# Products of ones in the waits of the head, slot constants computed earlier, and another order of ScalarE's work in the steps, in an attention and expert layer

## The reference

```
xn = layernorm(x)
q, k, v = xn Wq' + bq, xn Wk' + bk, xn Wv' + bv
pq, pk = elu(q) + 1, elu(k) + 1
x = x + (pq * cumsum(pk * v over tokens) / 4) Wo' + bo
xn = layernorm(x)                            # router, experts, shared part read this
top2 of xn @ router_w (8 experts); scores = softmax(top2 logits)
routed = sum over the two experts e of
         score_e * (silu(xn @ w1[e][:, :512]) * (xn @ w1[e][:, 512:])) @ w2[e]
shared = (silu(xn @ w_gate) * (xn @ w_up)) @ w_down       # 1024 wide
out = x + routed + shared
```

## Time and profile before

| | us |
|---|---|
| median of 3 runs | 373.13 (371.63 to 373.34) |
| the profiled execution | 372.15 |
| its span, first to last instruction | 370.4 |
| PE busy | 338.9 (91%) |
| DVE busy | 235.4 (64%) |
| ACT busy | 214.4 (58%) |
| POOL busy | 191.4 (52%) |
| mean granted TensorE clock | 0.984 |

### The profile page before, as it was taken

How to read it: one execution, slowest core, us unless ns; L and a number is a source line. 1 busy time by engine, 2 the same in 40 slices (tenths; PEclk the granted TensorE clock), 3 DMA queues, 4 the chain that set the end, 5 groups by cost and what they waited for, 6 DMA issues and landing times.

```text
span 370.4 us, 9019 instructions
## 1 busy us (share of the span) xinstructions
PE 338.9 (91%) x2868; PEld 251.9 (68%) x2868; DVE 235.4 (64%) x579; ACT 214.4 (58%) x389; POOL 191.4 (52%) x293
## 2 busy tenths in 40 slices
PE   6966698999997999999999899999999999999980
PEld 6755477887885887898888455656655556666650
DVE  4989976696984986887788556454545534443430
ACT  3778639776794776965535444454554554545440
POOL 4823185587786775948143641554343543434332
PEclk9999899999999899999999999999999999999997
DMA  6986162337374563455876345967595777686530
GB/s 186 388 206 202 25 123 73 74 88 230 61 183 159 116 198 75 118 186 160 242 238 157 87 70 92 92 92 105 79 105 84 102 108 83 103 99 96 77 48 0
DMA packets 77467, 46.41 MB, mean 125 GB/s; under 512 B 61040, under 2 KB 72560, under 8 KB 77040
## 3 DMA queue, kind: packets, MB, share of 16 engines
q1 hardware_dynamic: 63088, 35.08, 37.8%
q0 software_dynamic: 9664, 10.71, 19.0%
q10 hardware_dynamic: 4672, 0.07, 1.3%
HBM read 19.09 MB, written 12.97 MB: 87 GB/s over the span
## 4 chain that ended last, share of the span: by engine, by line
PE 51%; POOL 18%; DVE 12%; issue 10%; ACT 5%; DMA 1%; POOLq 1%; DVEq 0%; ACTq 0%
PE bU L1029 13%; PE bG L1029 12%; PE bV L1050 7%; POOL x_rows L571 6%; PE bQ L1050 6%; PE bD L927 3%; PE bU L238 3%; PE bG L238 2%; PE bK L1009 2%; DVE ab L1479 2%; DVE st L1356 2%; POOL y L486 1%; PE bV L238 1%; PE bK L238 1%; ACT xn L1122 1%
## 5 line engine op out<-in xcount | busy, mean ns | idle before, releaser
L1479 DVE SCALAR_TENSOR_TENSOR ab<-bU,sg 128x512 f32<-128x512 f32 x64 | 44.1, 690 | 77.2 <-PE bU L1029 51.3
L762 POOL DMA_INDIRECT out_y<-xs,dst_row x32 | 50.0, 1562 | 62.5 <-DMA out_y<-xs,dst_row 37.5
L1162 ACT ACTIVATE sg<-bG 128x512 f32<-128x512 f32 x64 | 37.9, 592 | 45.4 <-PE bG L1029 26.4
L1029 PE MATMUL bG<-we,work 128*128 (+1 forms) x216 | 52.6, 380 | 0.9 <-DVE wd L1535 0.9
L1029 PE MATMUL bU<-we,work 128*128 (+1 forms) x216 | 52.6, 379 | 0.0
L571 POOL DMA_INDIRECT x_rows<-rows,slot_u x32 | 38.3, 1198 | 21.0 <-DVE slot_u L1530 10.4
L1306 ACT ACTIVATE ws_h<-ab 128x512 f16<-128x512 f32 x36 | 22.7, 629 | 41.5 <-DVE ab L1479 41.5
L1169 ACT ACTIVATE ah<-ab 128x512 f16<-128x512 f32 x32 | 20.1, 628 | 32.7 <-DVE ab L1479 27.7
L1759 DVE TENSOR_TENSOR ws_h<-ab,ws_h 128x512 f16<-128x512 f32 x36 | 24.9, 693 | 20.8 <-ACT ws_h L1306 18.5
L1029 PEld LDWEIGHTS bG<-we,work 128*128 128x128 f16 (+1 forms) x216 | 20.7, 99 | 20.4 <-issue 2.8
L1029 PEld LDWEIGHTS bU<-we,work 128*128 128x128 f16 (+1 forms) x216 | 19.8, 99 | 17.4
(11 more groups left out here) (323 smaller groups left out, 811.0 us busy)
## 6 DMA issues: line engine op xcount, KB each, us to landing
stage<-in_w_expert SPq DMA_DIRECT2D x24, 512.0 KB
we<-in_w_shared SPq DMA_DIRECT2D x3, 1024.0 KB, 11.0
xs<-bo POOLq DMA_DIRECT2D x8, 256.0 KB, 4.1
out_y<-xs SPq DMA_DIRECT2D x8, 256.0 KB, 3.6
xs<-in_x SPq DMA_DIRECT2D x1, 1280.0 KB, 18.2
x_rows<-we SPq DMA_DIRECT2D x9, 134.0 KB
xs<-in_x SPq DMA_DIRECT2D x3, 256.0 KB, 3.8
work<-x_rows SPq DMA_TRANSPOSE x40
```

The lines of the kernel that those rows point to most:

```text
L762: pool.indirect_dma_start(out_rows, bass.IndirectOffsetOnAxis(ap=dst_row[:, b:b + 1], axis=0), ya[b % NY], None, bounds_check=NT * P - 1, ...
L1029: ins = pe.matmul(dst[t * n:(t + 1) * n, :], x2[:, hi * KC + k, t * n:(t + 1) * n], w[t][lo][:, k, half, :], start=s == 0 and k == 0, stop ...
L1162: act.activation(sg[q][:], src[:], ACT.Silu, scale=1.0 / WS).then_inc(S["sg_done"], 1)
L1479: dve.scalar_tensor_tensor(out=ab[q][:], in0=src[:], scalar=1.0 / WS, in1=sg[q][:], op0=ALU.mult, op1=ALU.mult).then_inc(S["a_done"], 1)
```

## The change

The diff, with the code that only gives it context cut:

```
 GpSimd
             add_bo(1)
             norm1(2)
+            slot_constants(0)
             pow2(0)
             add_bo(2)
+            slot_constants(1)
             norm1(3)
             pow2(1)
             gaps(0)
+            slot_constants(2)
             add_bo(3)
             add_taken(0)
             to_rows(0)
...
             gaps(1)
             add_taken(1)
+            slot_constants(3)
             to_rows(1)
             for i in range(3, B):
...
-                if i < 7:
-                    slot_constants(i - 3)
                 to_rows(i - 1)
 TensorE
-            def warm(n):
+            def warm(n, dst=bR):
                 for _ in range(n):
-                    pe.matmul(bR[:, 0:P], ones16[:], ones16[:], start=True, stop=True)
+                    pe.matmul(dst[:, 3 * P:4 * P], ones16[:], ones16[:], start=True, stop=True)
...
   in project(2), ahead of the third pass:       + warm(12, bQ)
   in attend_out(1), ahead of the third pass:    + warm(10)
   in gate_up, n = 2, m = 0, ahead of the third: + warm(16, bT)
             warm(48)
             pe.wait_ge(S["const_pool"], 4)
+            pe.wait_ge(S["pow1"], 1)
+            warm(10)
             turn_first(0)
+            warm(8)
             project(0, "kv")
             turn_first(1)
+            warm(7)
             project(0, "q")
             project(1)
+            warm(16)
             attend_out(0)
             turn_first(2)
+            warm(8, bQ)
             project(2)
+            warm(10)
             attend_out(1)
+            warm(22)
             route(0)
             pe.wait_ge(S["const_pool"], 6)
             gate_up(0, 0)
             gate_up(0, 1)
+            warm(20, bD)
             ranks(0)
...
   in expert_down:
                 pe.wait_ge(S["ath_done"], b + 1)
+                if b == 0:
+                    pe.wait_ge(S["ex_lo"], 3 * E)
   ahead of the blocks:
-            pe.wait_ge(S["ex_lo"], 3 * E)
+            pe.wait_ge(S["ex_lo"], 3 * E - 1)
             for b in range(NBLK):
 ScalarE, in every step
                 act_hi(j, 0)
+                silu(n + 1, 1)
+                act_hi(j, 1)
                 if i < B - 1:
                     normed1(i + 1)
-                silu(n + 1, 1)
-                if i < B - 1:
                     row_hi1(i + 1)
-                act_hi(j, 1)
                 expert_hi(part_of_step(i, first + 1))
 ScalarE, behind the steps, last piece of batch 7
             silu(n + 3, 1, bK)
+            expert_hi(part_of_step(B, 6))
             act_hi(j, 3)
-            expert_hi(part_of_step(B, 6))
 VectorE, the same place
             expert_lo(part_of_step(B, 5))
+            swiglu(n + 3, 1, bV)
             act_lo(j, 2)
-            swiglu(n + 3, 1, bV)
             act_lo(j, 3)
```

More of the change, by code:

```diff
@@ L805, in project @@
                             if s == 2:
+                                if i == 2:
+                                    warm(12, bQ)
                                 pe.wait_ge(S["l1_done"], i + 1)
@@ L826, in attend_out @@
                     if s == 2:
+                        if i == 1:
+                            warm(10)
                         pe.wait_ge(S["cxl_done"], i + 1)
@@ L889, in gate_up @@
                             if s == 2:
+                                if n == 2 and m == 0:
+                                    warm(16, bT)
                                 pe.wait_ge(S["sh_lo"], 3 * (n // 2) + m + 1)
```

11 lines of the change are left out of this document (6 added, 5 removed).

## The result

The changed kernel took 366.97 us (median of 4 runs, 366.93 to 367.03), the kernel before beside it 373.08 (371.63 to 373.34): ratio 0.984, 95% interval 0.982 to 0.987, 6.1 us less. The forecast was 367.1. The profiled execution took 367.03 us with a span of 365.3, 5.1 less than before.

The account below looks back on a forecast made before the run. TensorE was taken as full but with holes ahead of the blocks. Gains of 3.54 + 1.36 + 0 + 0 + 1.15 = 6.05 us gave 367.1 us from the 373.13 median, range 364.9 to 370.8.

Parts of the forecast that it names:

- Step 5 and step 6: Two stretches of TensorE's products ahead of the blocks: silu no longer late, gaining 3.54 us and 0.86 us.
- Start of the blocks: First expert product no longer waits for weight part 23, last `ab` comes earlier: 1.15 us gained (0.8 to 1.3).
- Steps 3 and 4: Two earlier stretches of TensorE's products: short waits ahead of the last up-product go, about 0.25 us gained in each.
- The fourth quarter: Last slot constants, ahead of `to_rows(1)` in the head: slip of 1.6 us, up to 2.3, costing TensorE 0 to 0.6.
- each with 1 us or more to spare: GpSimd's head: slot constants of 2.5 and 5.4 us fit into idle times of 4.73 and 6.52 us.
- 2.2 + 1.7 = 3.9: ScalarE from `act_hi(j, 1)` to the silu of piece 2: 3.9 us with the moved norm, some 0.8 us to spare.
- my 0.6: Upper bound on TensorE's loss if rstd slips 2.3 us and the silu of piece 2 comes late; 0 was taken.
- the 1.1 us that I had said would stay: Excess of step 4 ahead of the moved instructions, at the first silu: 1.1 us, not gained.
- Products of ones: 139 filling matmuls in TensorE's holes, to hold the clock: worth 0, bounds -0.3 and +1.7 us.
- my upper bound of 1.7: Most the filling matmuls could gain, if all the low-clock stretch from 40 to 45 us counted: 1.7 us.
- the second (a new wait on ScalarE): Silu of piece 2 about 1 us late in each of steps 3 to 6, some 3.5 us lost: 370.6 us; chance 0.14.
- the fourth: Slower: late rstd holds ScalarE at the norm with the silu of piece 2 behind it: 374.3 us; chance 0.05.

Follow-up runs that it names:

- the second trace: The changed kernel itself, unaltered, measured and traced again: 367.49 us.
- first quarter later: Changed kernel with the first quarter of slot constants behind pow2(0) and add_bo(2): 366.93 us; with the exp table also loaded early, 366.52 us.
- start of blocks back: Changed kernel with the waits and the two swaps at the start of the expert blocks undone: 367.79 us.
- the last variant: Changed kernel with the exp table loaded early and the fourth quarter of slot constants ahead of add_bo(3): 368.21 us.

## Why the prediction was right, and where it was not

**Step 5 and step 6: right.** 3.85 and 0.76 gained for 3.54 and 0.86 forecast. No low clock, rstd ahead of its reader, the silu of piece 2 in time. The prediction gave either edit the whole of step 5's gain, counted once. For the constants that holds (3.49 alone); ScalarE's order alone gives 1.92.

**Start of the blocks: right**, 1.06 for 1.15, and shown by its own variant (1.07).

**Steps 3 and 4: wrong in size, together 0.46 lost for 0.5 gained.** The fourth quarter, where I looked for the loss, was just in time as forecast: it took 3.2 us, and `to_rows(1)` started at 60.99, 0.95 behind VectorE's `slot_u`, where before, with nothing in between, it was 0.91. Two other steps of the prediction failed.

First, "each with 1 us or more to spare" for the first two quarters, which put their cost in the head at nothing. They cost 0.61 us between pow2(0) and the first row write (24.13 against 23.52; 23.52 again with the constants back): 0.55 of it is VectorE waiting for pow2(0), and when the first quarter is moved away from there, the two quarters hold up norm1(3) instead (24.36). The second took 6.2 us (26.72 to 32.90) instead of 5.4. I had found the two inputs in SBUF and the rule for them, and applied them to the fourth quarter only. The Trainium skill (SBUF — State Buffer, Who interferes with whom) has the rule; the trace agrees that the two slow each other, with 1.75 us against 0.71 for pow2(0) and 0.73 against 0.21 for `shift`, and in the second pair the later one is the slow one, as the rule says. In the first pair the slow one starts 0.01 us ahead, which is too little to tell who came first. In the first trace of the changed kernel the stall of step 3 grew from 0.93 to 2.12 because the step started 0.73 us earlier behind the row write and norm2(2) took 0.45 longer; behind it the clock fell, which is 1.22 us on one product.

Second, "2.2 + 1.7 = 3.9" us between `act_hi(j, 1)` and the silu of piece 2, with 0.8 to spare. From the end of the one to the start of the other it is 4.96 us in step 3 of the first trace, 4.82 in step 5 and 5.96 in step 3 of the second trace. The sum leaves out that the moved norm delays GpSimd's bias DMA, `dlog` behind it and `choice`, which waits 0.9 to 1.6 us. The list of what waits behind a moved instruction must go on through the other engine's list and back. In seven of the traces this is a stall of 1.06 or 1.07 in step 3, above my 0.6.

In step 4 the error has the other sign, 1.23 for 0.25: of the 1.1 us that I had said would stay, the stall ahead of the first silu (0.92 before) is gone wherever the constants are in the head, and is 0.74 where they are back in the steps. (The constants are 35 instructions, 8, 11, 4 and 12; the prediction's 39 counts a neighbour in each stretch. No term hangs on it.)

**Products of ones: 0 forecast, right in the sum and wrong in the reason.** I priced them against the head of before, where they are worth nothing (23.52 with and without). In the head that the change itself makes, the row write comes 1.23 us later without them, and the medians are 1.1 to 1.6 us apart, near my upper bound of 1.7; how much of the 1.23 reaches the end the traces leave open, since step 3 gives most of it back. The wait for `ws_l` did grow from 0.99 to 1.64, as forecast for 40 to 45 us, and the two variants with the first quarter later show that a low clock there costs nothing; what mattered lay at 34 to 38. The Trainium skill's price for a low clock (TensorE: Matmul & The Clock Gate, HAM oscillation), half of the throttled time, would give 1.7 for the 3.4 us at 40 to 45 of before; there the traces disagree, with nothing gained. Without fillings, from 34 to 38 us, a clock of 0.59 is 3.3 us at the lower level, so by the Trainium skill some 1.6, an estimate, against the 1.23 measured.

The hit on the median was partly luck. Between the profiled executions the gain is 5.12, 0.93 less than the sum of 6.05: 1.94 less than forecast in step 3 and 0.28 in the head, step 6 and the start of the blocks, against 0.98 more in step 4 and 0.31 in step 5. Against 372.15 the prediction had 366.1, and the profiled execution took 367.03. The medians are 6.1 apart because before's profiled execution lay 0.98 below its median and the changed kernel's did not. Of the rivals, the second (a new wait on ScalarE) is true in step 3 alone, with 1.06 us in seven traces, and the fourth only with the constants in the steps.

## What to carry to other kernels

Work moved into an engine's idle time is free only if no busy engine beside it slows it (the fourth quarter took 3.2 or 6.7 us), it slows no one else, and nothing behind it was already on the path: follow the delay to the end, and price fillings against the holes of the new order, not of the old. When an instruction is moved back in one list, look for who waits for it with something urgent behind, and move that ahead; here one such swap and one table load put into a wait gave 2.0 to 2.5 us more. And look at a second execution before explaining a stall: one stall here had two forms in the same program, and only the variants beside it showed which wait set its length.

## What the runs showed of the hardware

- GpSimd's pow2(0), 128x2 elements, took 0.71 us when it started 0.1 ahead of VectorE's scan (23.94 and 24.04) and 1.75 when it started 0.01 ahead (24.15 and 24.16). Moving the first quarter of the constants decided which. GpSimd's `shift`, as small, took 0.21 when it started 0.06 ahead of VectorE's `al` (56.68 and 56.74, start of blocks back) and 0.73 when it started 0.02 behind (56.91 and 56.89); that is 0.6 us of TensorE's stall.
- TensorE's clock and the stall ahead of it: it stayed at 1.00 behind 0.93, 1.53 and 1.87 us of standing still, and fell behind 2.12 (0.68 over 65 to 70 us) and 2.27 (0.69, the last variant), as it had in step 5 of before behind 1.95. In the head it fell at 42 us with the fillings in place, behind 1.50 us (first quarter later). What else it depends on these runs don't tell.
- ScalarE's last silu of the head started 1.7 us after its product in most traces and at once in some others, in the changed kernel itself once so and once so, with no engine named as releaser. In the trace of the changed kernel in which it is late, step 3 starts 0.66 us later behind the row write. The cause stays open; nothing here tests it.
